# Decoder block: cross-attention keys and values from halves of the context, and one pair of output buffers for both attentions

## The reference

```
x = layernorm(x + self_attention(x))            # qk-norm, rope, causal
x = layernorm(x + cross_attention(x, ctx))      # causal and key mask
x = layernorm(x + ffn(x))                       # light 128 + heavy 1024 hidden units
K = ctx @ Wk; V = ctx @ Wv                      # the products that the change touches
scores = Q K^T / 4 (+ masks); out = softmax(scores) V; out @ Wo
```

## Time and profile before

| | us |
|---|---|
| median of 3 executions | 1029.55 (1028.53 to 1033.22) |
| the profiled execution, its own time | 1031.08 |
| span in its profile, first to last instruction | 1029.3 |
| TensorE busy | 921.1 (89%) |
| VectorE busy | 734.1 (71%) |
| ScalarE busy | 490.1 (48%) |
| GpSimd busy | 466.4 (45%) |

### The profile page before, as it was taken

The page is one execution under the profiler, slowest core; times in us unless marked ns, Lnnn a source line. Parts: engine busy times, 40 slices in busy tenths (PEclk is TensorE's granted clock), DMA queues, the critical chain, the costliest instruction groups (busy, mean ns, idle before and its releaser), DMA issues.

```text
span 1029.3 us, 21587 instructions
## 1 busy us (share of the span) xinstructions
PE 921.1 (89%) x7776; PEld 711.1 (69%) x7776; DVE 734.1 (71%) x1843; ACT 490.1 (48%) x1047; POOL 466.4 (45%) x883
## 2 busy tenths in 40 slices
PE   2565898899999999999999999999999999998886
PEld 2333565587877778786878777787868786766675
DVE  8645858687787877777878878777777788563612
ACT  1131161645555564636465555546374655445343
POOL 2150454545546363546455564635464554233221
PEclk9666799999999999999999999999999999999989
DMA  3629356554729183554546280937556462804000
GB/s 104 82 70 148 63 63 79 79 74 70 97 48 106 39 107 61 81 87 64 84 75 93 52 116 24 110 57 89 79 64 95 62 85 47 111 13 64 21 1 21
DMA packets 79643, 74.22 MB, mean 72 GB/s; under 512 B 8592, under 2 KB 78896, under 8 KB 79536
## 3 DMA queue, kind: packets, MB, share of 16 engines
q1 hardware_dynamic: 75872, 68.90, 46.6%
q10 hardware_dynamic: 3664, 3.94, 1.7%
HBM read 17.49 MB, written 4.20 MB: 21 GB/s over the span
## 4 chain that ended last, share of the span: by engine, by line
PE 61%; DVE 17%; issue 9%; POOL 4%; ACT 3%; DMA 3%; ACTq 1%; SPq 0%; POOLq 0%; DVEq 0%
PE bank L342 56%; PE bank L367 4%; DVE mx L869 3%; POOL pr L1176 3%; DMA y<-in_b 2%; ACT pr L728 2%; DVE x L946 1%; DVE rest L853 1%; DVE y L918 1%; DVE st L925 1%; DVE ss L971 1%; DVE nat2q L858 1%; DVE on L909 1%; DVE rden L906 1%; ACT sq L815 1%
## 5 line engine op out<-in xcount | busy, mean ns | idle before, releaser
L728 ACT ACTIVATE pr<-bank 128x384 f32<-128x384 f32 x512 | 242.5, 499 | 205.5 <-PE bank L342 205.2
L869 DVE TENSOR_REDUCE mx<-bank 128x3 f32<-128x384 f32 x512 | 268.6, 552 | 92.8 <-PE bank L342 89.2
L1176 POOL TENSOR_SCALAR_AFFINE_SELECT pr<-pr 128x256 f32<-128x256 f32 x512 | 225.3, 448 | 214.6 <-ACT pr L728 210.8
L342 PE MATMUL bank<-w,g 128*128 128x256 f32 x576 | 170.8, 389 | 1.1 <-ACT g L740 1.1
L342 PE MATMUL bank<-cmaskb,idb 128*128 128x256 bf16 x512 | 145.7, 285 | 28.5 <-DMA stk1k<-nat1k 14.6
L740 ACT ACTIVATE g<-bank,b 128x256 f32<-128x256 f32 x144 | 68.3, 475 | 112.3 <-PE bank L342 111.8
L1200 POOL TENSOR_TENSOR xTlow<-xT,xThigh 128x512 fp32r<-128x512 f32 x16 | 21.2, 1327 | 174.7 <-ACT xThigh L674 174.7
L342 PEld LDWEIGHTS bank<-w,g 128*128 128x128 f32 x576 | 89.6, 190 | 5.2 <-ACT g L740 1.5
L342 PE MATMUL bank<-stk1k,stk1q 97*128 97x128 bf16 (+1 forms) x512 | 88.6, 259 | 0.0
L342 PEld LDWEIGHTS bank<-cmaskb,idb 128*128 128x128 bf16 x512 | 50.4, 98 | 52.6 <-DVE mx L869 22.2
L342 PE MATMUL bank<-stk1q,stk1k 100*128 100x256 bf16 (+1 forms) x512 | 79.9, 254 | 4.5 <-DMA stk1q<-mT 3.1
(11 more groups left out here) (143 smaller groups left out, 1792.1 us busy)
## 6 DMA issues: line engine op xcount, KB each, us to landing
stk1q<-nat1q SPq DMA_DIRECT2D x96, 128.0 KB, 4.7
stk1k<-nat1k SPq DMA_DIRECT2D x96, 128.0 KB, 6.7
stk2k<-nat2k SPq DMA_DIRECT2D x96, 128.0 KB, 4.6
stk2q<-nat2q SPq DMA_DIRECT2D x96, 128.0 KB, 6.1
xT<-in_xT SPq DMA_DIRECT2D x16, 256.0 KB, 2.8
x<-in_x SPq DMA_DIRECT2D x16, 256.0 KB, 6.8
ctxT<-in_ctxT SPq DMA_DIRECT2D x16, 256.0 KB, 3.0
out_x<-x SPq DMA_DIRECT2D x16, 256.0 KB, 6.5
```

The source lines that it names most:

```text
L342: return nc.tensor.matmul(out, lhsT, rhs, start=start, stop=stop, skip_group_check=check)
L728: nc.scalar.activation(pr[:, h % (2 * HG), :], ring_bank("T", a, b, h)[:, 0:3 * P], ACT.Exp, scale=HD ** -0.5)\
L869: V.tensor_reduce(mx3[:, h, :], scored[:, 0:3 * P].rearrange("p (k t) -> p k t", k=3), AX.X, ALU.max, negate=True).then_inc(s_mx[a], 1)
L1176: G.affine_select(out=slot, in_=slot, compare_op=ALU.is_ge, fill=0.0, base=0, pattern=[[0, 2], [1, P]], channel_multiplier=-1).then_inc(s_ ...
```

## The change

Cross keys and values are made from halves as the self projections are. The weights `wk2` and `wv2` are loaded raw into the unused part of `pr` and split once by VectorE (`halve_cross`). For each element ScalarE makes `ctxhigh` (`high_ctx`, placed behind `high_x`), GpSimd makes `ctxlow` (placed behind `xTlow`), and `k2` waits for `ctxlow` where it waited for the load. The load of `ctxT` waits for `ctxlow` of the element before. Both attentions write one `oT` and one `on`; each writer waits until the other attention's reader is done.

```diff
-        wq2 = sb("wq2", [P, C, D]); wk2 = sb("wk2", [P, C, D]); wv2 = sb("wv2", [P, C, D])
+        wk2 = [sb(f"wk2{part}", [P, C, D], f32r) for part in ("high", "low")]
+        wv2 = [sb(f"wv2{part}", [P, C, D], f32r) for part in ("high", "low")]
...
+        wk2raw, wv2raw = [staged[:, n * C * D:(n + 1) * C * D].rearrange("p (c n) -> p c n", c=C) for n in (3, 4)]
@@ SyncE, step @@
-                    wait(sp, s_v[2], s)
+                    wait(sp, s_clow, s)
                     load(ctxT[:, :, :], dims(io["ctxT"], s), s_ctxT)
@@ TensorE, k2 and v2 @@
-                    pe.wait_ge(s_wcross, 16 * N_CROSS)
-                pe.wait_ge(s_ctxT, 16 * (b + 1))
+                    pe.wait_ge(s_chalf, 4)
+                pe.wait_ge(s_clow, b + 1)
...
-                for c in range(C):
-                    last = dim_proj(bank[SPLIT_BANK[2][1]][:, c * T:(c + 1) * T], wk2, c * P, ctxT)
+                for m in range(C):
+                    out = bank[SPLIT_BANK[2][1]][:, m * T:(m + 1) * T]
+                    products = [(w, x, c) for w, x in ((wk2[0], ctxp[0]), (wk2[0], ctxp[1]), (wk2[1], ctxp[0])) for c in range(C)]
+                    for n, (w, x, c) in enumerate(products):
+                        last = mm(out, w[:, c, m * P:(m + 1) * P], x[:, c, :], n == 0, n == len(products) - 1)
...
-                    last = tok_proj(bank[V_BANK[2]][:, t * D:(t + 1) * D], ctxT, t, wv2, 0, D)
+                    last = halves_proj(bank[V_BANK[2]][:, t * D:(t + 1) * D], ctxp, t, wv2)
@@ ScalarE, copy_group, high_ctx and step @@
+                if a == 1:
+                    wait(act, s_ott[2], TT * (b - 1))
+                else:
+                    wait(act, s_ott[1], TT * (b + 2) if live(b + 1) else TT * B)
+                copy(oT[:, gr, :], bank[OT_BANK][:, 0:T]).then_inc(s_oT[a], 1)
...
+            def high_ctx(b):
+                act.wait_ge(s_ctxT, 16 * (b + 1))
+                wait(act, s_v[2], b)
+                copy(ctxp[0][:, :, :], ctxT[:, :, :]).then_inc(s_chigh, 1)
...
                     high_x(i + 2)
+                if live(s):
+                    high_ctx(s)
@@ VectorE, normalise_heads, step and halve_cross @@
+                    if a == 1:
+                        wait(dve, s_ont[2], b - 1)
+                    else:
+                        wait(dve, s_ont[1], b + 2 if live(b + 1) else B)
...
                 if first(i + 1):
+                    halve_cross()
                     more_rows()
...
+            def halve_cross():
+                dve.wait_ge(s_wcross, 16 * N_CROSS)
+                for n, (w, raw) in enumerate(((wk2, wk2raw), (wv2, wv2raw))):
+                    V.tensor_copy(w[0][:, :, :], raw).then_inc(s_chalf, 1)
+                    dve.wait_ge(s_chalf, 2 * n + 1)
+                    V.tensor_tensor(w[1][:, :, :], raw, w[0][:, :, :].bitcast(f32), ALU.subtract).then_inc(s_chalf, 1)
@@ GpSimd, step @@
+                if live(s):
+                    pool.wait_ge(s_chigh, s + 1)
+                    wait(pool, s_v[2], s)
+                    G.tensor_tensor(ctxp[1][:, :, :], ctxT[:, :, :], ctxp[0][:, :, :].bitcast(f32), ALU.subtract)\
+                        .then_inc(s_clow, 1)
```

More of the change, by code:

```diff
@@ L80, in build @@
         wo1 = sb("wo1", [P, C, D])
-        wq2 = sb("wq2", [P, C, D]); wk2 = sb("wk2", [P, C, D]); wv2 = sb("wv2", [P, C, D])
+        wq2 = sb("wq2", [P, C, D])
+        wk2 = [sb(f"wk2{part}", [P, C, D], f32r) for part in ("high", "low")]
+        wv2 = [sb(f"wv2{part}", [P, C, D], f32r) for part in ("high", "low")]
         wo2 = sb("wo2", [P, C, D])
@@ L94, in build @@
         xT = sb("xT", [P, C, T]); xTp = [sb(f"xT{part}", [P, C, T], f32r) for part in ("high", "low")]
-        ctxT = sb("ctxT", [P, C, T]); x1T = sb("x1T", [P, C, T])
+        ctxT = sb("ctxT", [P, C, T]); ctxp = [sb(f"ctx{part}", [P, C, T], f32r) for part in ("high", "low")]
+        x1T = sb("x1T", [P, C, T])
         xnh = sb("xnh", [P, C, T], f32r); xnl = sb("xnl", [P, C, T], f32r)
@@ L121, in build @@
         pr = sb("pr", [P, 2 * HG, 3 * P])
-        oT = [None] + [sb(f"oT{a}", [P, NG, T]) for a in (1, 2)]
+        oT = sb("oT", [P, NG, T])
         rden = [None] + [sb(f"rden{a}", [P, TT, H]) for a in (1, 2)]
-        on = [None] + [sb(f"on{a}", [P, TT, D]) for a in (1, 2)]
+        on = sb("on", [P, TT, D])
         onT = [None] + [sb(f"onT{a}", [P, C, T]) for a in (1, 2)]
@@ L151, in two @@
             return [None, sem(name + "1"), sem(name + "2")]
-        s_xhigh = sem("xT_high_ready"); s_xlow = sem("xT_low_ready"); s_whalf = sem("self_weights_halved")
+        s_xhigh = sem("xT_high_ready"); s_xlow = sem("xT_low_ready"); s_whalf = sem("self_weights_halved"); s_chalf = sem("cross_weights_halved"); s_chigh = sem("ctx_high_ready"); s_clow = sem("ctx_low_ready")
         s_wqk1 = sem("wqk1_loaded"); s_wself = sem("self_weights_loaded"); s_wcross = sem("cross_weights_loaded"); s_wffn = sem("ffn_weights_loaded")
@@ L563, in out_tokens @@
                         last = nc.tensor.transpose(bank[TOK_BANK[a][t]][:, gr * P:(gr + 1) * P],
-                                                   oT[a][:, gr, t * P:(t + 1) * P], idf[:, :])
+                                                   oT[:, gr, t * P:(t + 1) * P], idf[:, :])
                     last.then_inc(s_ott[a], 1)
@@ L570, in out_dims @@
                     pe.wait_ge(s_rest[2], 2 * b + 1)
-                four_transposes(DIM_BANK[a], on[a]).then_inc(s_ont[a], 1)
+                four_transposes(DIM_BANK[a], on).then_inc(s_ont[a], 1)
             def out_proj(a, b):
@@ L695, in copy_group @@
                 wait(act, s_ott[a], TT * b)
-                copy(oT[a][:, gr, :], bank[OT_BANK][:, 0:T]).then_inc(s_oT[a], 1)
+                if a == 1:
[3 more added lines that the diff above has]
+                copy(oT[:, gr, :], bank[OT_BANK][:, 0:T]).then_inc(s_oT[a], 1)
             def copy_x1(b):
@@ L827, in _ @@
             chunks = "(c p) n -> p c n"
-            for w, name in ((wo1, "wo1"), (wk2, "wk2"), (wv2, "wv2"), (wq2, "wq2"), (wo2, "wo2")):
+            for w, name in ((wk2raw, "wk2"), (wv2raw, "wv2"), (wo1, "wo1"), (wq2, "wq2"), (wo2, "wo2")):
                 load(w[:, :, :], io[name].rearrange(chunks, p=P), s_wcross)
@@ L908, in normalise_heads @@
                     wait(dve, s_ont[a], b)
-                    V.tensor_tensor(on[a][:, t, :].rearrange("p (h d) -> p h d", d=HD), o[:, :, 0:HD],
+                    if a == 1:
+                        wait(dve, s_ont[2], b - 1)
+                    else:
+                        wait(dve, s_ont[1], b + 2 if live(b + 1) else B)
+                    V.tensor_tensor(on[:, t, :].rearrange("p (h d) -> p h d", d=HD), o[:, :, 0:HD],
                                     rden[a][:, t, :].rearrange("p (h o) -> p h o", o=1).to_broadcast([P, H, HD]),
```

## The result

The changed kernel took 1044.04 us in the median of three runs (1042.41 to 1048.42), against 1029.55: ratio 1.0141 [1.0079, 1.0203]. It is slower, as forecast, but by about twice as much: + 14.5 us in the medians, and in the profiled span, which went from 1029.3 to 1042.3 us, + 13.0, where the sum said + 7.1.

The account below looks back on a forecast made before the run. TensorE, busy 89% of the span, was taken as the bound. - 7.7 (matmuls) + 7.0 (border, steps 3 to 12) + 7.8 (first three steps) = + 7.1, forecast 1036.7 us against the median 1029.55; range for 8 in 10: 1028 to 1042.

Parts of the forecast that it names:

- The gain of TensorE: Cross values and cross keys blocks shorten to 1.52 us each: 0.48 us per element, 7.7 us over 16 elements.
- The wait at the border: Between second and third phase, TensorE's first self values wait for late masks: 0.7 us in steps 3 to 12, 7.0 us.
- its own sign: At the first self values: the prediction is wrong if TensorE's wait for masks is under 0.4 us.
- VectorE's delay is used up before the next place where it is waited for: Behind the border: VectorE's layer norm 2 comes 1.0 us later, but costs nothing beyond the 0.7 us wait.
- The first three steps: Steps 0 to 2, without TensorE feed-forward work, lose 3.4, 2.1 and 2.3 us at the values; together 7.8 us.
- The edits at nothing: Splitting the raw cross weights and sharing oT and on cost nothing; without cover the split costs 2 us once.
- Rival 1: At the first self values: new work falls into ScalarE's and GpSimd's idle time, so faster, 1021.9 us; chance 0.10.
- Rival 3: At the border: longest landing every step, VectorE's delay reaches the transposes of xn; + 16, 1046 us; with rival 4 0.08.
- my case: TensorE's gain is outweighed by waits at the border and in the first three steps; 1032 to 1041 us; chance 0.68.
- rival 4: In cross keys and values: halves don't speed TensorE up among bf16 heads; 1044 us; together with Rival 3 0.08.
- Rival 2: The border wait is there but taken back later in the step, so no change: + 0.1, 1029.7 us; chance 0.14.
- The prediction's 2.6 us for the load: Load of ctxT: skill's estimate of about 2.0 us fixed plus 256 KB at 436 GB/s; the sum used measured 3.0 us.

Follow-up runs that it names:

- e5: Changed kernel, but ctxhigh and ctxlow made for element 0 only and read for all elements' cross keys and values; 1024.13 us, ratio 0.9952 to the kernel before.
- e1: Changed kernel, but SyncE issues the load of ctxT ahead of that of xT; 1021.04 us, ratio 0.9945 to the kernel before.
- e7: Changed kernel, but ctxlow is a plain copy of ctxT instead of the difference; 1036.58 us, ratio 1.0053 to the kernel before.
- e4: Changed kernel, but ctxlow on GpSimd stands behind x1c and rstd, still ahead of the masks; 1037.9 us, ratio 1.0061 to the kernel before.
- e2: Kernel before, with only the shared oT and on and their waits added; 1029.82 us, ratio 1.0011 to the kernel before.
- e3: Changed kernel without the raw weights' split and the matmuls from halves; ctxhigh and ctxlow made but unused; 1048.56 us, ratio 1.019 to the kernel before.
- e9: e4 with the transposes of the cross maxima one head later on TensorE; 1037.66 us, ratio 1.0085 to the kernel before.
- e8: Changed kernel with one small unused load more on SyncE ahead of ctxT; 1045.92 us, ratio 1.0131 to the kernel before.
- e6: e1 with the first ctxT loaded ahead of the loop and ctxlow behind x1c and rstd; 1022.99 us, ratio 0.991 to the kernel before.

## Why the prediction was right in direction and off in size

**The gain of TensorE.** The blocks were right to 0.01 us. Around them 0.10 us more per step is saved; e5 shows that 0.58 us per step arrives in the middle steps. The term was 7.7, and is 9.3.

**The wait at the border.** The chain was right, each link by the views that the prediction had named: `ctxhigh` idle on the landing, `ctxlow` 0.7 us behind, `x1c` and `rstd`, then masks, none of it in steps 13 to 15. The typical size was right too, 0.69 us against 0.7, and so was the length of `ctxlow` (1.27 us). That the size agrees is in part luck: the prediction put all of it down to masks, and of the 0.69 only 0.28 is a wait for them. By its own sign, a wait for masks under 0.4 us, it would have been wrong. But the term for steps 3 to 12, 7.0, measured 11.8:
- I took the median landing for the mean. Two of ten landings are near 4 us, 1 us above the median, and each is paid in full: the mean border wait is 0.91, 2.1 us more in all. The earlier trace rows had shown the 3.8; in the kernel before, a landing had over 10 us to spare and its scatter cost nothing. What goes with the late ones is in the last section. I used it for the range alone, and there said that steps don't all take an extreme. That is so, but they don't average to the median either.
- "VectorE's delay is used up before the next place where it is waited for" is the step that failed. I looked for a place where VectorE's results are waited for. It was still 0.4 us late at the twelfth mask, which reads nothing of VectorE's and is slowed beside it: 0.27 us per step, 2.7 in all. In e1, where VectorE is on time (the subtraction at 521.65, the mask at 522.31), the mask takes 0.41 us; in e7, where VectorE is late, 0.69. The effect has a dose: over steps 3 to 12 of all twelve traces, 120 masks, the mask takes 0.41 us in the 50 where VectorE's subtraction ends at most 0.13 us after the mask's start, and in the 70 where it ends 0.17 to 0.44 us after it, the mask ends 0.26 to 0.27 us behind the subtraction.
- The same sentence didn't reckon with a delay of VectorE ahead of layer norm 2, the 1.17 us copy. In the changed kernel 0.27 us of the border stands at `mp` for it; had it been without, the masks would have held the first values nearly as long. It is why mending the masks alone (e4) gives back so little.

**The first three steps.** 7.8 predicted, 9.8 measured. At the first values I had 3.4, 2.1 and 2.3, and the traces show 3.2, 2.7 and 3.2: 9.1. Step 2 is the largest miss at that place, since I took the loss at its second values, which had waited before, and not at the first, which hadn't. The last 0.7 us are the balance of larger parts. At `xThigh` of steps 0, 1, 2 and 3 the changed kernel is 0.8 us ahead, then 1.2, 5.0 and 8.0 behind. With the 0.58 us gained added back, step 0 costs 2.6, less than its 3.2, and VectorE's wait for the feed-forward weights is 1.7 us shorter; step 1 costs 4.3, 1.7 more than its border, of which 0.7 stand before its third values and 1.0 in no wait read here, where the lower clock is the likely place; step 2 costs 3.6. The prediction left the clock out.

**The edits at nothing.** The shared buffers (e2) are free. For the weights' split nothing can be seen either way: `xThigh` of step 0 starts at 57.94 us in the changed kernel, 58.84 in its second trace and 58.73 before, and in the two traces without the split, e2 and e3, at 57.53 and 60.58, a scatter larger than the 2.8 us at stake.

**The rivals.** Rival 1, faster because the work falls into idle time, named its own condition: the load must land 0.7 us earlier. e1 is that rival made true by moving one load by 4.1 us; the idle times of ScalarE and GpSimd do hold the work. Rival 3 had the mechanism that did the rest (long landings, VectorE), but the landings in every step, and VectorE's delay at the transposes of `xn` and not beside a mask. The result lies between my case and rival 3, nearer to rival 3. It is also the very 1044 of rival 4, by chance: e5 shows that the halves do speed TensorE up. Rival 2 falls too, since the step is 56.8 us and nothing of the wait is taken back.

The Trainium skill (GPSIMD Engine Reference, Key points) says that GpSimd shares its path to the memory with VectorE and contends with VectorE instructions that have two inputs there or run in a two-port mode. Which of the two waits, that section doesn't say; the prediction read it as a `ctxlow` that takes longer. The traces agree on the contention, and the later starter pays: `ctxlow` keeps its 1.27 us and the small VectorE copy waits it out (1.17 us), while a mask beside a two-input VectorE operation is the one that grows (0.41 to 0.68 us). The small copy has one input; whether it runs in a two-port mode, no trace shows.

The prediction's 2.6 us for the load comes from a section of the Trainium skill (DMA: Bandwidth & Descriptors, Anatomy of one DMA) that is about transfers issued by GpSimd. `ctxT` is issued by SyncE, and its sixteen loads took 2.7 to 4.2 us here.

## What to carry to other kernels

A copy that is placed in idle time costs nothing only if its input is there in time: follow the input back to where its load is issued, and move that load first. Where a transfer that had slack becomes awaited, charge the mean of its landings with the late ones in it, not the median. And behind a delayed engine look not only at who waits for it, but at what it now lies beside; when two chains end close together, mending one shows the other. Before a difference is put down to waits, compare the granted clock stretch by stretch.

## What the runs showed of the hardware

A VectorE instruction of 16 or 32 columns can take 0.92 to 1.29 us instead of 0.17 to 0.19 beside a GpSimd subtraction with two inputs of 128x512 (1.27 to 1.33 us): in the 59 cases of six traces it starts beside that and ends 0.03 to 0.05 us behind its end. In groups of 32 such copies, busy us and mean ns, before, after and in e4:

```profile
L882 DVE COPY nm<-mx 128x16 f32<-128x16 f32 x32 | 5.7, 180 | 1.1
```
```profile
L902 DVE COPY nm<-mx 128x16 f32<-128x16 f32 x32 | 11.5, 360 | 1.1
```
```profile
L902 DVE COPY nm<-mx 128x16 f32<-128x16 f32 x32 | 12.9, 404 | 1.1
```

Beside the plain copies of e7, 0.61 us each, short VectorE instructions took 0.45 to 0.63 us, and ended as close behind. A mask of 256 columns took up to 0.70 us instead of 0.41 beside a VectorE subtraction of 512 columns, and ended 0.26 to 0.27 us behind that.

The same 256 KB load lands after 2.5 to 4.8 us. In six traces with the load behind `xT` (the changed kernel twice, e4, e5, e7, e9) steps 11 and 12 have landings of 3.7 to 4.2 us, in e8 3.4 and 3.5, in e3 2.9 and 3.0. The DMA queues tell the late ones apart. While the load of step 12 of the changed kernel is under way, 753.7 to 757.9 us, the profile shows one packet more than for that of step 8, 16 KB on a queue of instructions:

```profile
q8 instruction: 1, 0.02, 2.1%
```

In the ten traces with the load behind `xT` there are 130 such loads. In 19 of them a 16 KB packet of instructions is in flight: 18 land after 3.36 to 4.20 us, and one, whose packet ends 0.07 us after the issue, after 3.01. The other 111 land after 2.72 to 3.22 us, but for one of 3.52. So steps 11 and 12 are late where such a packet falls on them, and in e3, where it falls on step 5, that step has the landing of 3.60. In e1 and e6, with `ctxT` first, four loads with a packet that starts 1.0 to 1.2 us after the issue land after 3.9 to 4.8 us, and eight with an earlier packet after 2.7 to 3.0. No run moves the packet alone, so this is a regularity of the traces; that the packet is the cause is likely and not shown.
